# Attention by column groups of TensorE, row sums on GpSimd, and a second graph mix laid out by token

## The reference

```python
# x: (64, 128, 128), adj: (128, 128), 4 heads of 32 features
h = relu(layernorm(x))
q, k, v = split(h @ W)                       # per head
attn = softmax(q @ k.T / sqrt(32) + where(adj == 0, -inf, 0))
x = x + attn @ v
h = relu(layernorm(x))
h = relu(adj @ (h @ Wg0 + bg0))
h = relu(adj @ (h @ Wg1 + bg1))
for p in 1, 2, 3, 4:                         # LSTM over windows of p tokens
    h[:, last token of each window] = lstm_p(windows of h)
x = x + h
```

## Time and profile before

| what | value |
|---|---|
| median of 3 runs | 535.61 us (533.58 to 540.34) |
| the profiled execution's own time | 539.53 us |
| its span in the profile | 537.7 us |
| mean granted TensorE clock | 0.981 |
| busy: PE, PEld | 503.2 us (94%), 436.8 us (81%) |
| busy: DVE, ACT, POOL | 409.7 (76%), 347.1 (65%), 150.4 (28%) |

### The profile page before, as it was taken

How to read it: one execution, slowest core, us unless ns; L and a number is a source line. 1 busy time by engine, 2 the same in 40 slices (tenths; PEclk the granted TensorE clock), 3 DMA queues, 4 the chain that set the end, 5 groups by cost and what they waited for, 6 DMA issues and landing times.

```text
span 537.7 us, 9995 instructions
## 1 busy us (share of the span) xinstructions
PE 503.2 (94%) x3464; PEld 436.8 (81%) x3464; DVE 409.7 (76%) x929; ACT 347.1 (65%) x561; POOL 150.4 (28%) x167
## 2 busy tenths in 40 slices
PE   3788999999999999999997899999999999999994
PEld 3587888888888888888886777888999987888884
DVE  3856667887779777887767578888888888986875
ACT  2454566866677666866666777777776666665551
POOL 2434044425453354425011001211112122222211
PEclk9986999999999999999998999999999999999998
DMA  7322000000000000000000000000000000000225
GB/s 213 111 80 83 17 1 2 2 0 0 0 0 0 0 0 0 0 0 0 2 1 1 1 1 0 2 0 0 2 1 1 0 2 0 1 0 1 79 79 156
DMA packets 18778, 11.29 MB, mean 21 GB/s; under 512 B 662, under 2 KB 17724, under 8 KB 18748
## 3 DMA queue, kind: packets, MB, share of 16 engines
q1 hardware_dynamic: 17052, 10.03, 6.6%
q10 hardware_dynamic: 1696, 0.87, 0.6%
HBM read 6.70 MB, written 4.19 MB: 20 GB/s over the span
## 4 chain that ended last, share of the span: by engine, by line
PE 69%; DVE 14%; ACT 8%; issue 5%; DMA 2%; POOL 1%; DVEq 1%; ACTq 0%; SPq 0%; POOLq 0%
PE ps L894 25%; PE ps L830 10%; PE ps L739 7%; PE ps L750 7%; PE ps L843 3%; DVE S_hi L1208 3%; PE ps L771 3%; PE ps L787 3%; PE ps L848 2%; DVE arena L1195 2%; PE ps L761 2%; PE ps L936 2%; ACT arena L563 2%; ACT arena L577 2%; ACT arena L585 2%
## 5 line engine op out<-in xcount | busy, mean ns | idle before, releaser
L599 ACT ACTIVATE arena<-ps,bias 128x512 f32<-128x512 f32 (+1 forms) x207 | 121.2, 625 | 45.3 <-PE ps L894 43.7
L563 ACT ACTIVATE arena<-ps 128x512 f32<-128x512 f32 (+1 forms) x112 | 85.5, 790 | 54.8 <-PE ps L750 45.9
L543 POOL TENSOR_TENSOR arena<-arena 128x512 f32<-128x512 f32 (+1 forms) x36 | 43.2, 1201 | 180.0 <-ACT arena L599 180.0
L894 PE MATMUL ps<-H_hi,W_hi 128*128 128x512 f32 (+2 forms) x207 | 75.6, 365 | 3.4 <-DVE S_lo L1210 2.1
L830 PEld LDWEIGHTS ps<-arena 128*128 128x128 f32 x512 | 65.8, 196 | 12.4 <-issue 8.2
L894 PE MATMUL ps<-H_lo,W_hi 128*128 128x512 f32 (+2 forms) x207 | 74.9, 362 | 0.0
L894 PE MATMUL ps<-H_hi,W_lo 128*128 128x512 f32 (+2 forms) x207 | 74.8, 361 | 0.0
L830 PE MATMUL ps<-arena 128*128 128x33 f32 x512 | 65.1, 273 | 3.1 <-ACT arena L563 1.6
L510 POOL TENSOR_TENSOR veps<-mv,eps 128x4 f32<-128x4 f32 x32 | 11.7, 365 | 191.0 <-DVE mv L1064 191.0
L520 POOL TENSOR_SCALAR arena<-X,mv,rstd 128x128 f32<-128x128 f32 x56 | 59.9, 1080 | 1.5
L739 PE MATMUL ps<-ident,arena 128*128 128x128 f32 x384 | 52.7, 287 | 7.5 <-POOL arena L520 2.7
(11 more groups left out here) (105 smaller groups left out, 988.2 us busy)
## 6 DMA issues: line engine op xcount, KB each, us to landing
X<-in_x_dram SPq DMA_DIRECT2D x16, 256.0 KB, 2.8
out_dram<-X SPq DMA_DIRECT2D x14, 256.0 KB, 2.4
out_dram<-X ACTq DMA_DIRECT2D x2, 256.0 KB, 3.9
arena<-in_L_gnn_W_dram ACTq DMA_DIRECT2D x1, 128.0 KB, 3.1
wg<-in_L_gnn_Wg_dram ACTq DMA_DIRECT2D x2, 64.0 KB, 2.4
bg_rows<-in_L_gnn_bg_dram SPq DMA_DIRECT2D x6, 0.5 KB
wv<-in_L_gnn_W_dram ACTq DMA_DIRECT2D x1, 64.0 KB, 3.2
adj_sb<-in_adj_dram SPq DMA_DIRECT2D x1, 64.0 KB, 3.3
```

What stands on the lines that cost most here:

```text
L543: g_.tensor_tensor(ig[:, it.buf, 0:w], sig_i[:, it.buf, 0:w], tanh_g[:, it.buf, 0:w], ALU.mult)\
L563: a_.activation(to, psum, func).then_inc(ready, 1)
L599: a_.activation(to[:, it.buf, 0:w], ps[:, 4 * it.par + j, 0:w], func, bias=bias[:, col:col + 1])\
L894: l = mm(o, wt, v, start=m == 0, stop=m == len(terms) - 1)
```

## The change

- `attend` takes all four heads at once. The stationary operand is now the values (128x32) and the moving one the transposed probabilities (128x128); each head writes its own 32 partitions of one PSUM bank (`psO`), so it uses its own 32 columns of the array. The result has features in partitions. There are still 16 f32 matmuls in a group.
- ACT copies that bank into `att` (`read_att`), TensorE transposes it back with 4 transposes (`attended`, into bank 5, `psR`), and DVE divides and adds to `X` in `add_attention`, which has moved to the next iteration, between `shift` 0 and `moments` 1.
- The column of ones is gone. POOL halves the exponentials three times per two heads (`add_halves`: 64, 32 and 16 sums of each row), and DVE reduces the last 16 (`over_sums`).
- The orders change: DVE's `normalize` now comes ahead of `shift` 1; TensorE's first graph mix ahead of `project` of k, and `transpose_prob(s, 1)` behind `graph_linear_1`; ACT's copy of `hn2` ahead of `read_hT`, its copy of `u1T` ahead of `first_gate` 0.
- The second graph mix writes PSUM token by token, and `u2T` is copied in one run.

```diff
@@ POOL
+            def add_halves(s, half):
+                n = s.k * 2 - 1 + half
+                part = slice(2 * half * GB, 2 * (half + 1) * GB)
+                pv = prob.rearrange("p (c n) -> p c n", n=N)[:, part, :]
+                pool.wait_ge(exp_ready, n)
+                g_.tensor_tensor(by_64, pv[:, :, 0:N // 2], pv[:, :, N // 2:N], ALU.add).then_inc(by_64_ready, 1)
+                pool.wait_ge(by_64_ready, n)
+                g_.tensor_tensor(by_32, by_64[:, :, 0:N // 4], by_64[:, :, N // 4:N // 2], ALU.add)\
+                    .then_inc(by_32_ready, 1)
+                pool.wait_ge(by_32_ready, n)
+                if s.back:
+                    pool.wait_ge(sums_row, s.k - 1)
+                g_.tensor_tensor(by_16[:, part, :], by_32[:, :, 0:N // 8], by_32[:, :, N // 8:N // 4], ALU.add)\
+                    .then_inc(by_16_ready, 1)
             def iteration(s):
                 if s.back:
                     rsqrt(1, s.k - 2, var2, veps2, rstd2)
+                if s.mid:
+                    add_halves(s, 0)
+                    add_halves(s, 1)
                 if s.next2:
                     rsqrt(0, s.k + 2, var1, veps1, rstd1)
                     first_norm(s.k + 2)
@@ ACT, iteration
+                read(hn2, hn2, xn2_ready, k - 1, hn2_ready, ACT.Relu)
                 if s.next1:
                     read_hT(psX[s.back], k + 2, 1 - s.par)
+                read(u1T[:], psA, u1_done, k - 1, u1T_ready)
                 if s.finish:
...
                     first_gate(k - 3, 0, act_i, 0, 0.5)
-                read(hn2, hn2, xn2_ready, k - 1, hn2_ready, ACT.Relu)
                 if s.mid:
                     exp(s, 1)
...
-                read(u1T[:], psA, u1_done, k - 1, u1T_ready)
...
-                read(by_token_batch_first(u2T), batches(psA), u2_done, k - 1, u2T_ready)
+                read_att(s)
+                read(u2T[:], psA, u2_done, k - 1, u2T_ready)
@@ TensorE
-            def attend(s, half):
...
+            def attend(s):
+                pe.wait_ge(probT_ready, s.k * 2)
+                for b in range(GB):
+                    at_ = slice(b * N, (b + 1) * N)
+                    for h in range(HEADS):
+                        l = mm(psO[h * HD:(h + 1) * HD, at_], v_sb[:, 1 - s.par, b, h, :], probT[:, h, at_],
+                               start=True, stop=True)
+                l.then_inc(att_done, 1)
+            def attended(s):
+                pe.wait_ge(att_read, s.k)
+                transposed(psR, batches(att)).then_inc(attT_done, 1)
@@ TensorE, iteration
                 first_gate(s, 0, 0)
-                if s.mid:
...
-                    interleave([], attend(s, 0))
...
                 interleave([], graph_mix(hn2, u1_done))
-                if s.mid:
-                    transpose_prob(s, 1)
+                if s.front:
+                    if s.next1:
+                        pe.wait_ge(hT_hi_ready, k + 2)
+                    pe.wait_ge(x2_ready, k - 1)
+                    interleave([], project(s, psK, D, k_done))
...
                 graph_linear_1().then_inc(z1_done, 1)
+                if s.mid:
+                    transpose_prob(s, 1)
                 first_gate(s, 1, 2)
                 if s.front:
+                    pe.wait_ge(probT_ready, k * 2 - 1)
                     put_mask((0, 1))
                     pe.wait_ge(probT_ready, k * 2)
+                    put_mask((2, 3))
+                    pe.wait_ge(q_ready, k + 1)
                     pe.wait_ge(k_ready, k + 1)
-                    masks = [lambda h=h: put_mask((h,)) for h in (2, 3)]
-                interleave(attend(s, 1), masks)
+                attend(s)
                 if s.front:
                     scores()
+                attended(s)
                 pe.wait_ge(h1_ready, k - 1)
-                interleave([], graph_mix(h1, u2_done))
+                interleave([], graph_mix(h1, u2_done, by_token_batch_first(psA)))
                 first_gate(s, 2, 3)
@@ DVE
+            def over_sums(s):
+                dve.wait_ge(by_16_ready, s.k * 2)
+                v_.tensor_reduce(row_sums[:], by_16, AX_X, ALU.add).then_inc(sums_row, 1)
+                dve.wait_ge(sums_row, s.k)
+                v_.reciprocal(rec[:], row_sums[:]).then_inc(rec_ready, 1)
+            def add_attention(k):
+                dve.wait_ge(rec_ready, k - 1)
+                dve.wait_ge(attT_done, k - 1)
...
+                v_.tensor_tensor(by_head(att_n), by_head(psR), ..., ALU.mult).then_inc(att_scaled, 1)
+                dve.wait_ge(att_scaled, k - 1)
+                xg = X[:, ds(k * GB - 2 * GB, GB), :]
+                v_.tensor_tensor(xg, xg, batches(att_n), ALU.add).then_inc(x2_ready, 1)
+                dve.wait_ge(x2_ready, k - 1)
+                moments(1, k - 2, stats2, var2)
@@ DVE, iteration
                 if s.mid:
                     shift(s, 0)
                 if s.back:
-                    dve.wait_ge(x2_ready, 2 * k - 2)
-                    moments(1, k - 2, stats2, var2)
+                    add_attention(k)
...
+                if s.back:
+                    normalize(1, k - 2, xn2, rstd2, xn2_ready)
                 if s.mid:
                     shift(s, 1)
...
-                if s.mid:
-                    over_sums(s, 0)
...
                 if s.mid:
-                    over_sums(s, 1)
+                    over_sums(s)
```

More of the change, by code:

```diff
@@ L274, in gnn_block @@
         act_i, act_g, act_o, u1T = take(GT), take(GT), take(GT), take(GT)
+        att_n = take(GT)
+        by_32 = take(GT // 2).rearrange("p (c n) -> p c n", n=N // 4)
+        by_16 = take(GT // 2).rearrange("p (c n) -> p c n", n=N // 8)
         assert at[0] <= ARENA
@@ L305, in gnn_block @@
         psX = {True: psK, False: psB}
-        psO = ps[:, 4:6, :]
+        psO, psR = ps[:, 4, :], ps[:, 5, :]
         def psW(m):
@@ L647, in read_v, with read_att @@
                 if s.back:
-                    act.wait_ge(att_done, 2 * s.k - 2)
-                a_.activation(v_sb[:, s.par, :, :, 0:HD], psA.rearrange("p (b h d) -> p b h d", b=GB, h=HEADS),
+                    act.wait_ge(att_done, s.k - 1)
+                a_.activation(v_sb[:, s.par, :, :, :], psA.rearrange("p (b h d) -> p b h d", b=GB, h=HEADS),
                               ACT.Copy).then_inc(v_ready, 1)
+            def read_att(s):
+                read(att, psO, att_done, s.k, att_read)
             def fill(s):
@@ L821, in transpose_prob @@
                 l.then_inc(probT_done, 1)
-            def attend(s, half):
-                def part(b):
-                    if b == 0:
-                        pe.wait_ge(probT_ready, s.k * 2 - 1 + half)
-                    for h in (2 * half, 2 * half + 1):
-                        o = b * 2 + h % 2
-                        l = mm(psO[:, half, o * (HD + 1):(o + 1) * (HD + 1)], probT[:, h, b * N:(b + 1) * N],
-                               v_sb[:, 1 - s.par, b, h, :], start=True, stop=True)
-                    if b == GB - 1:
-                        l.then_inc(att_done, 1)
-                return [lambda b=b: part(b) for b in range(GB)]
+            def attend(s):
[9 more added lines that the diff above has]
+                transposed(psR, batches(att)).then_inc(attT_done, 1)
             def scores():
@@ L976, in fill @@
                     pe.wait_ge(k_ready, k + 1)
-                    interleave(attend(s, 1), [lambda h=h: put_mask((h,)) for h in (2, 3)])
+                    put_mask((2, 3))
+                    attend(s)
                 else:
@@ L1137, in shift @@
                     .then_inc(shifted, 1)
-            def over_sums(s, half):
-                dve.wait_ge(att_done, s.k * 2 - 1 + half)
-                v_.reciprocal(rec4[:, half], o4[:, half, :, :, HD]).then_inc(rec_ready, 1)
-                dve.wait_ge(rec_ready, s.k * 2 - 1 + half)
-                v_.tensor_tensor(att5[:, half], o4[:, half, :, :, 0:HD],
-                                 rec4[:, half].unsqueeze(3).to_broadcast([P, GB, 2, HD]), ALU.mult).then_inc(att_read, 1)
-                dve.wait_ge(att_read, s.k * 2 - 1 + half)
-                heads = slice(half * 2 * HD, (half + 1) * 2 * HD)
-                xg = X[:, ds(s.k * GB - GB, GB), heads]
-                v_.tensor_tensor(xg, xg, att.rearrange("p (b d) -> p b d", b=GB)[:, :, heads], ALU.add)\
-                    .then_inc(x2_ready, 1)
+            def over_sums(s):
[6 more added lines that the diff above has]
+                dve.wait_ge(attT_done, k - 1)
+                by_head = lambda T: T.rearrange("p (b h d) -> p h b d", b=GB, h=HEADS)
+                v_.tensor_tensor(by_head(att_n), by_head(psR),
+                                 rec[:].rearrange("p (h b) -> p h b", h=HEADS).unsqueeze(3)
+                                 .to_broadcast([P, HEADS, GB, HD]), ALU.mult).then_inc(att_scaled, 1)
+                dve.wait_ge(att_scaled, k - 1)
[3 more added lines that the diff above has]
+                moments(1, k - 2, stats2, var2)
             def first_cell_part(g):
```

(2 more changed lines are left out.)

46 lines of the change are left out of this document (23 added, 23 removed).

## The result

The changed kernel takes 579.91 us (median of 4 runs, 577.75 to 581.98). The kernel before, run beside it on the same chip, takes 537.92. The ratio is 1.079, 95% interval [1.072, 1.086]: slower by 42 us, where 550 was forecast, with a range to 570. The profiled execution has a span of 575.9 us and a mean granted clock of 0.950; before it was 537.7 and 0.981. Executions of the kernel before fall in two groups, one around 535 us at a mean clock of 0.99 and one around 539 at 0.98, and the profiled one is of the second, so the two spans differ by 38.2 us and not by 42.

A forecast was written before the change was run, and what follows sets the result against it. TensorE's own work bounds the kernel now; after the change a ring through all engines does. 14 iterations by +1.1 us (+15.4) and about 1 us gained in the fill make +14.4: 550 us median, range 529 to 570.

The forecast's parts named there:

- TensorE's own work: Per iteration on TensorE: old attend -3.5 us, new attend +1.1, attended +0.4, leaving 14.5 us of work.
- The upper bound of 3.5 us for groups one behind the other: Rival at attend: column groups run serially, 3.5 us instead of 1.1, giving 568 or 584 us; chance 0.08.
- The ring: Line of waits through all engines from scores to the next scores: 10.22 us to the first mix plus 7.04, 17.26 us.
- 3 us taken off TensorE: Work removed from TensorE per iteration, said to become waiting ahead of the first mix, 1.8 us idle there.
- the hold: POOL's add_halves 0 holds DVE's normalize through the shared port: +1.1 us an iteration; rival without it 535 us, chance 0.25.
- The upper bound of 2.4: Most that normalize could be delayed per iteration, in us, if held for all three POOL sums.
- The clock: Rival: TensorE's clock falls behind the wait ahead of the first mix, 14 x 1.6 = +22 us; chance 0.17.
- the likeliest case: The forecast itself, pipeline with +1.1 us an iteration: 550 us, own range 545 to 556, chance 0.36.
- The fill and the end: Iterations outside the full pipeline: the fill gains about 1 us, iterations 16 and 17 come to 0.
- The signs named beforehand: In the trace: iteration 18.4 us, PE waiting 1.8 to 2.9 ahead of the mix, first L1070 1.4, clock near full.
- The copy of u2T: ACT's copy falls from 1.09 to 0.6 us, worth nothing since TensorE has 1.8 us to spare behind it.
- The faster side: Rival: TensorE stays the bound, iteration 14.5 to 15.5 us, 503 us; decides from a ring of 16.5; chance 0.14.

The follow-up runs named there:

- serial groups: The version with wait and fillers, with the four heads of the attention taken one after the other (head outside, batch inside): 559.75 us, ratio 1.045.
- the run where the halves wait: The changed kernel, but POOL waits for DVE's normalize before add_halves 0: 543.62 us, ratio 1.010.
- the 12 fillers: The changed kernel with 12 bf16 mask matmuls into a free bank ahead of TensorE's wait for hn2: 566.56 us, ratio 1.056.
- wait and fillers: The changed kernel with POOL waiting for normalize before add_halves 0, and six mask matmuls ahead of TensorE's wait for hn2: 538.12 us, ratio 1.002.
- the reordered versions: Wait and fillers, with scores ahead of attend, exp 1 ahead of the first gate, row sums ahead of first_cell_part: 527.54 us without fillers, 524.99 with six.
- the fastest version: The one of the reordered versions that keeps the six fillers: 524.99 us, ratio 0.980 against the kernel before.

## Why the prediction was right or wrong

**TensorE's own work:** right for the parts that changed. `attend` took 1.08 us where 1.1 was taken, and `attended` 0.49 to the start of the next (175.99 to 176.48) where 0.4 was. The upper bound of 3.5 us for groups one behind the other was not what serial groups cost; they took 2.46.

**The ring:** right, and not by luck of the sum. 17.26 us was the sum of its steps, 17.38 the bare ring; its two parts, 10.22 us from `scores` to the first mix and 7.04 from there, measured 10.25 and 7.13 in the run where the halves wait. The "3 us taken off TensorE" do not fit the prediction's own terms, which give 3.5 - 1.1 - 0.4 = 2.0, and without the hold the wait ahead of the first mix was 1.35 us and not 1.8. That this work would turn into waiting there was right, and the serial groups show the other half of it, that a microsecond added on the ring is a microsecond of the iteration.

**The hold: right in its mechanism, mis-sized.** The term was 1.1 us and measured 1.77. I let only the first sum hold `normalize` and wrote that "the rest of the halving then has to wait in turn". It does not: `normalize` is four short instructions, each sum of POOL gets in between two of them, and each holds one. The starts of the four show what each is worth, against the 0.26 us from start to start that four in 1.11 us have: 184.24 - 183.02 = 1.22 for the first, 0.80 and 0.53 for the next two. That is 0.96 + 0.54 + 0.27 = 1.77. The upper bound of 2.4 had all three sums in it end to end; what is missing to it is `normalize`'s own work, which is done beside them. Over 14 iterations this is 14 x 1.77 = 24.8 us instead of 15.4: 9.4 us of the miss. That the hold, with the fall of the clock behind the wait it makes, stood between 580 and 544 is shown by the single wait. The Trainium skill, SBUF — State Buffer, section "Who interferes with whom", says that whoever issues first has the shared ports for the whole instruction. The trace agrees for each instruction by itself (1.28 us of POOL, 1.30 for the first `normalize`). What the sum needed besides, that the turn goes back and forth between the short instructions of both engines, the rows above show.

**The clock: a rival that should have been part of the forecast.** I had the clock fall in every iteration as a case of 0.17 and 22 us, beside the hold. It was no case of its own. The wait that the hold lengthens is the one behind which the clock falls: with the hold PE stood 3.09 us and the clock fell in 12 of 14 iterations; without it 1.35 us, and in the steady iterations it did not. So the two come together. Its price was smaller than the 1.6 us an iteration that I took from iteration 16: 0.8 on the mean, for two reasons. Where the clock fell it cost about 1.0 us, 20.21 - 19.15 = 1.06 in the iteration shown. The lower level did not last shorter there: windows of half a microsecond have it from 187.7 to 191.2, about as long as the 3.4 us of the earlier trace rows. But at full speed TensorE has a wait of some 0.3 us between `graph_linear_1` and the transposes (they start 1.19 us behind L808 in the iteration from 75.00, where its 8 matmuls need 0.9), and the slower L808 runs into it; the rest of the difference is open. And in two iterations the clock did not fall. Over 14 iterations the 12 fillers take 278.58 - 267.36 = 11.2 us away. In the first iteration the clock falls in spite of them (0.91, and 1.00 with wait and fillers); there the two versions differ by 3.16 us and everywhere else by the 1.77 of the hold, so 1.4 us more are the clock's. That makes 12.6 us which the likeliest case did not have. The length of the wait alone does not decide it: before the change the clock fell behind 1.41 us, here it stayed up behind 1.35, and within the changed kernel the same 3.09 us were followed by a fall in some iterations and by none in two. What decides it is open.

**The fill and the end.** The fill gained 2.6 us and not 1. The end lost 5.2 and not 0: PE stood 3.17 us ahead of the mix of iteration 16, and 324 to 332 ran at 0.52 of the clock. From the last `scores` to the walk the changed kernel takes 26.03 us, the version with 12 fillers 326.87 - 303.12 = 23.75, the one with wait and fillers 299.78 - 277.81 = 21.97, and the kernel before 20.84. So 2.3 us of the loss at the end are the clock, 1.8 the hold, and 1.1 neither.

**The sum with the measured terms:** the 14 iterations take 242.91 us before, 241.16 with wait and fillers, 267.36 with fillers alone and 278.58 as changed. That is ring -1.7 (in its first full iteration the kernel before itself runs at a granted clock of 0.74), and hold and clock 267.36 - 241.16 + 11.2 = 37.4, of which 24.8 are the hold and 12.6 the clock; then fill -2.6 and end +5.2. Together 38.3, against 38.2 by the spans. Of the 24 us between the forecast of +14.4 and this, 9.4 are the size of the hold, 12.6 the clock, 3.6 fill and end together (+2.6 where -1 stood), and the ring takes 1.7 off. So two steps of the prediction failed: the hold, which was priced as one instruction of POOL's three, and the clock, which was left at nothing in the likeliest case.

**The signs named beforehand:** the hold of the first L1111 (1.30 us, 1.4 forecast) and the wait ahead of the first mix were there, the wait at 3.09 us a little over the 1.8 to 2.9. An iteration of 20.2 us instead of 18.4 and a clock of 0.92 instead of full were the two signs that did not come as the likeliest case had them.

**The copy of u2T:** "worth nothing" was right inside the change, which is only argued; alone on the kernel before it gave 0.16 us an iteration.

**The faster side.** The condition I gave, a ring under 16.5 us, was about right: the ring of the change as made is 17.38, and the reordered versions with 16.53 are 1.5 and 2.0% faster. The change takes some 2 us of work off TensorE in an iteration. As made, none of it comes through; with the halving away from `normalize`, `attend` off the ring and ScalarE's order changed, 17.27 - 16.53 = 0.74 us do.

## What to carry to other kernels

When work is moved to an engine that shares something with another, look at what its first instruction stands next to: an instruction that had been released by the same event gets held, and so does a short one behind it for each instruction that the newcomer has queued. One semaphore wait that lets the short critical instructions go first cost nothing here and was worth 34 to 36 us of 580, the clock's share included. And before an engine is relieved, add up the ring of waits that goes through all engines: if it is as long as the iteration, the relief turns into idle time, the idle time can cost the clock, and here gain came only when steps were taken out of the ring, as `attend` behind `scores` was.

## What was not expected of the hardware

- GpSimd's three `tensor_tensor` kept their own lengths (1.28, 0.72, 0.45 us) and held one each of DVE's four `tensor_scalar` of 128 columns, which take 0.34 us alone: both queues advanced in turn, and in this meeting only DVE paid. Beside DVE's `tensor_tensor` from SBUF the 512 columns took POOL 1.64 us, and both paid.
- Four column groups of f32 matmuls, 128x32 weights and 128 moving columns, ran at 34 ns an instruction and one group at 77 ns: 2.3 times, not four.
- The same wait of 3.09 us was followed by a fall of the clock in some iterations and by none in two, in one execution.
- Six filler bf16 matmuls of 1.5 us an iteration, whose result nobody reads, were worth 5.5 us with the wait on POOL (543.62 to 538.12) and 2.5 us in the fastest version, where the executions with and without them still overlap.
- Writing PSUM with a step of 4 elements cost the second mix nothing (1.06 us for 8 matmuls, 1.16 before).
